# The weights of an instruction planner: ScalarE barred from the general PSUM banks after the first scores, and all work ordered anew

## What is computed

```
x = x + attn(layernorm(x))               # 16 heads, q and k made of 6 "line" coordinates, causal
x = x + xattn(layernorm(x), ctx, ctx)    # 16 heads of 16, 1601 context rows
x = x + ffn(layernorm(x))                # 16 experts, 64 rows each, chosen by a sinkhorn router

# attn:  q1,q2 = [x, x_prev] @ W1_q.T, W2_q.T;  k1,k2 = x @ W1_k.T, W2_k.T
#        q = lines(q1,q2); k = lines(k1,k2)   (6 products of pairs, normalised)
#        softmax(q . J k / sqrt(6), causal) @ (x Wv.T + bv), then @ Wo.T + bo
# xattn: softmax(q . k) @ v, then @ Wo.T + bo
```

## Time and profile before

| | |
|---|---|
| median of 3 executions | 1175.59 us (1175.5 to 1178.8) |
| the profiled execution | 1176.3 us, its span 1174.6 us |
| TensorE busy | 1102.7 us (94%) |
| VectorE busy | 854.1 us (73%) |
| ScalarE busy | 728.2 us (62%) |
| GpSimd busy | 153.5 us (13%) |
| mean granted TensorE clock | 0.979 of full speed |

### The profile page before, as it was taken

How to read it: one execution, slowest core, us unless ns; L and a number is a source line. 1 busy time by engine, 2 the same in 40 slices (tenths; PEclk the granted TensorE clock), 3 DMA queues, 4 the chain that set the end, 5 groups by cost and what they waited for, 6 DMA issues and landing times.

```text
span 1174.6 us, 30371 instructions
## 1 busy us (share of the span) xinstructions
PE 1102.7 (94%) x12600; PEld 522.4 (44%) x12600; DVE 854.1 (73%) x1998; ACT 728.2 (62%) x842; POOL 153.5 (13%) x260
## 2 busy tenths in 40 slices
PE   4898988999999999999999999999999999888997
PEld 2452432332332233554455455555654543466454
DVE  4986366588767788789788889788888891368631
ACT  0355756778777887677776887678875789310111
POOL 3134224112111111000001000010000000000522
PEclk9997998999999999999999999999999999999999
DMA  5112277502011000104231301111101000088696
GB/s 168 59 50 78 91 102 136 114 23 74 10 44 46 15 15 2 52 16 114 62 104 56 98 17 29 52 48 30 29 15 58 30 16 3 24 286 216 189 349 163
DMA packets 81561, 90.44 MB, mean 77 GB/s; under 512 B 18208, under 2 KB 73952, under 8 KB 81424
## 3 DMA queue, kind: packets, MB, share of 16 engines
q1 hardware_dynamic: 75264, 80.04, 24.5%
q10 hardware_dynamic: 4368, 6.29, 1.7%
q0 software_dynamic: 1792, 2.16, 1.0%
HBM read 73.42 MB, written 15.04 MB: 75 GB/s over the span
## 4 chain that ended last, share of the span: by engine, by line
PE 79%; DVE 13%; issue 3%; ACT 2%; DMA 2%; POOL 1%; SPq 0%; ACTq 0%; DVEq 0%
PE po L1778 24%; PE g L1886 16%; PE scores L1754 14%; PE scores L1758 6%; PE g L1871 3%; PE g L1977 2%; PE g L2001 2%; ACT probs L1194 2%; PE g L1861 2%; PE g L1821 1%; PE g L1865 1%; PE g L1806 1%; DMA xb<-x_d 1%; DVE mx L1465 1%; PE g L1831 1%
## 5 line engine op out<-in xcount | busy, mean ns | idle before, releaser
L1194 ACT ACTIVATE probs<-scores 128x1024 f32<-128x1024 f32 (+2 forms) x736 | 677.7, 968 | 226.1 <-PE scores L1754 132.6
L1465 DVE TENSOR_REDUCE mx<-g 128x1 f32<-128x400 f32 (+1 forms) x1024 | 526.1, 568 | 88.1 <-PE g L1886 79.3
L1886 PE MATMUL g<-cross_region,even_region 96*32 96x400 bf16 (+1 forms) x4096 | 305.7, 336 | 0.9 <-DVE mx L1465 0.4
L1754 PE MATMUL scores<-even_region,cross_region 99*32 99x512 bf16 (+1 forms) x3264 | 254.6, 379 | 3.0 <-ACT probs L1194 3.0
L1778 PE MATMUL po<-probs,cross_region 128*32 128x512 f32 (+1 forms) x1664 | 224.8, 594 | 0.8 <-ACT probs L1194 0.8
L1886 PEld LDWEIGHTS g<-cross_region,even_region 96*32 96x32 bf16 x4096 | 121.4, 95 | 172.8 <-DVE mx L1465 68.2
L1778 PE MATMUL po<-probs,self_region 128*32 128x512 f32 (+3 forms) x1280 | 153.4, 554 | 5.9 <-POOL probs L1055 5.0
L1754 PEld LDWEIGHTS scores<-even_region,cross_region 99*32 99x32 bf16 (+1 forms) x3264 | 100.1, 96 | 95.0 <-issue 41.7
L1758 PE MATMUL scores<-self_region 36*128 36x512 bf16 (+3 forms) x640 | 107.2, 360 | 7.2 <-ACT probs L1194 6.7
L1022 POOL TENSOR_TENSOR rstd<-mv,half 128x1 f32<-128x1 f32 x48 | 28.2, 592 | 549.2 <-DVE mv L1273 549.1
L1055 POOL TENSOR_SCALAR_AFFINE_SELECT probs<-probs 128x256 f32<-128x256 f32 x128 | 60.8, 482 | 237.7 <-ACT probs L1194 236.6
(11 more groups left out here) (288 smaller groups left out, 886.7 us busy)
## 6 DMA issues: line engine op xcount, KB each, us to landing
cross_region<-in_w SPq DMA_DIRECT2D x16, 1024.0 KB, 13.3
even_region<-xq_d SPq DMA_DIRECT2D x192, 64.0 KB, 2.3
self_region<-in_w ACTq DMA_DIRECT2D x6, 1024.0 KB, 7.0
self_region<-in_w SPq DMA_DIRECT2D x6, 1024.0 KB, 13.1
cross_region<-xk_d SPq DMA_DIRECT2D x24, 200.1 KB, 8.5
xb<-in_x SPq DMA_DIRECT2D x32, 128.0 KB, 2.8
xb<-x_d SPq DMA_DIRECT2D x32, 128.0 KB, 2.2
probs<-in_w SPq DMA_DIRECT2D x4, 1024.0 KB, 13.9
```

The source lines that it names most:

```text
L1194: act.activation(probs[0:rows, s % 4, :, off:], ps[s % 2][0:rows, :, off:], ACT.Exp, scale=LSCALE if QUADS[n][0] == "self" else 1.0).then_ ...
L1465: dve.reduce_max(mx[:, k % 2, b, h, c:c + 1], g[:, 0:n_keys], AX_X).then_inc(g_free, 1)
L1754: mm = pe.matmul(ps[s % 2][c:c + n_keys, a, :], k_cross[0:NS * DH + 3, h, i * P + c:i * P + c + n_keys], rhs, start=True, stop=True)
L1886: mm = pe.matmul(g[q:q + 32, 0:n_keys], q_max[k % 2][0:NS * DH, h, b * P + q:b * P + q + 32], k_cross[0:NS * DH, 4 * (k % 4) + h, start:st ...
```

## The change

Twelve numbers of `W` are new; nothing else differs. `act_late` goes from 0.3 to 50, and after the first score step VectorE empties every general bank. `hungry`, `act_near`, `max`, `max_end`, `lines`, `ctx`, `keys`, `weights`, `start`, `late` and `act_early` were chosen anew with it.

```diff
--- before.py
+++ after.py
@@ -69,10 +69,10 @@
 NS = len(Q_SLOTS)
 
 
-W = dict(hungry=0.714, fed=0.0083, act_near=0.2211, max=3.7538, max_ahead=0.0147, max_from=72.59, max_end=8.352,
-         prep=0.7203, x=0.2428, lines=0.6125, ctx=0.2601, keys=0.054, early_ctx=0.2835, early_lines=3.9514,
-         early_x=2.8, ones=0.4536, query=0.5762, weights=0.0015, start=1.7136, late=0.9073, act_late=0.3,
-         act_early=0.01)
+W = dict(hungry=0.2498, fed=0.0083, act_near=0.2255, max=0.4357, max_ahead=0.0147, max_from=72.59, max_end=10.0224,
+         prep=0.7203, x=0.2428, lines=0.1574, ctx=0.1821, keys=0.0688, early_ctx=0.2835, early_lines=3.9514,
+         early_x=2.8, ones=0.4536, query=0.5762, weights=0.0036, start=0.5141, late=1.0888, act_late=50,
+         act_early=0.0026)
 
 
 def build_plan():
```

## The result

| | before | after |
|---|---|---|
| median of 20 executions each | 1176.37 us (1172.9 to 1179.2) | 1172.22 us (1169.4 to 1175.2) |
| ratio, 95% interval | | 0.9967 [0.9958, 0.9976] |
| the profiled execution, its span | 1176.3, 1174.6 us | 1175.17, 1173.4 us |
| TensorE, VectorE, ScalarE busy | 1102.7, 854.1, 728.2 us | 1105.5, 860.9, 718.2 us |

The change makes the kernel 0.33% faster, some 4 us, with the bound of 0.3% inside the interval. The forecast was 1175, no change. The profiled execution of the changed kernel is the slowest of its twenty. So a second profile, of the same kernel run again, is read beside it; its span is 1168.9 us and its own time 1170.6. It errs the other way: it is the fastest of the eleven executions of its run, whose median is 1173.2.

The account below looks back on a forecast made before the run. TensorE was taken as the bound from 220.9 to 950 us, with idle time and lower clock to win or lose ahead of it. Terms +2.6 + 2.7 - 4.1 + 1.2 - 3.1 + 0.2 = -0.5 us gave 1175 us, range 1167 to 1183.

Parts of the forecast that it names:

- Ahead of the first scores: Up to the first scores: they come 2.7 us earlier, but some 5.2 us of TensorE work is left; net +2.6 us.
- Line blocks of tile 1: First scores to tile 1's line blocks: fewer filling steps leave TensorE idle 4.6 us in place of 1.9; +2.7 us.
- 86 to 160 us: `lines(2,0)` and `lines(2,1)` still slow the diagonal quads' masks, so the 3.5 us values wait stays; 0, ±3 us.
- 160 to 221 us: `lines(3,2)` ahead of the query cuts removes the 2.5 us line-block wait and 1.6 us of query-block waits; -4.1 us.
- rival 1: 160 to 220.9 us: all 8.5 us idle and the 5.1 us of lower clock go; 1166 us, chance 0.32.
- Quads 56 to 59: First `max` comes six quads late, so these quads, diagonal at the group's end, have no filling; +1.2 us.
- Changes of shape: 22 fewer changes of TensorE's tile shape: -3.1 us if TensorE is the bound at all, 0 if at none.
- The moved copies: Twelve steps' copies behind the first scores go from ScalarE to VectorE, neither on the path; 0, bounds -2 and +2 us.
- signs of being wrong: TensorE waits over 3 us for L1339, L1350 or L1432 (100-190 us), or pre-221 us lower clock over 8 us off 23.9.
- signs that it named for being right: Include a first L1854 wait of 3 us or more, the masks' wait still there, `max` starting within 3 us of 221.
- A: Theory of the experiments: the gain comes from where tile 3's steps now stand, around 160 to 220 us; ratio 0.997.
- C: Theory of the experiments: the gain comes from 22 fewer changes of TensorE's tile shape; ratio 0.997.

Follow-up runs that it names:

- b1: Kernel before with only `lines(3,2)` moved ahead of both query cuts on VectorE: ratio 0.9989 [0.9978, 1.0001] to before.
- a1: Changed kernel, order held, ScalarE again emptying the twelve listed `project`, `x_turn` and `ctx_v` banks: ratio 0.9991 [0.9975, 1.0006] to before.
- a3: Changed kernel, order held, only `project` 9 to 11 and two `x_turn` given back to ScalarE: ratio 0.9978 [0.9964, 0.9992] to before.
- e1: Changed kernel with, from quad 60, `max` steps between a self quad's two score steps put behind the second: ratio 0.9986 [0.9972, 1.0000] to before.
- d1: Planned with the weights of before until values step 36, the new weights from there: ratio 0.9979 [0.9961, 0.9998] to before.
- r0: Changed kernel run again unchanged, as the level for the others: 1173.19 against 1177.34 us, ratio 0.9970 [0.9960, 0.9981] to before.
- a2: Kernel before, order held, VectorE emptying the twelve listed `project`, `x_turn` and `ctx_v` banks: ratio 1.0104 [1.0085, 1.0123] to before.
- b2: Changed kernel with only `lines(3,2)` moved back behind both query cuts on VectorE: ratio 1.0005 [0.9992, 1.0019] to before.
- c1: Kernel before with only `act_late` raised from 0.3 to 50 and the order planned anew: ratio 1.0382 [1.0367, 1.0397] to before.
- d2: Planned with the new weights until values step 36, the weights of before from there: ratio 1.0108 [1.0092, 1.0124] to before.

## Where the prediction was right and wrong, step by step

The range of 1167 to 1183 held, and so did the forecast's own, 1171 to 1179. Its value, no change, did not: the sum said -0.5 us, the median moved by -4.2 and the second profile by -5.7. That it lies no further off is in part luck. At the last cross scores, up to which the sum counts, the second profile leads by 8.2 us, 7.7 more than the sum; behind them the scatter of the clock takes 2.5 us back, and most executions are slower than this one. By the prediction's own steps, with the table of lags:

- **Ahead of the first scores, +2.6: right.** Measured +3.0. The first scores stand at 65.3 us (64.7 forecast), the two waits are 5.2 and 4.2 us (5.3 and some 4).
- **Line blocks of tile 1, +2.7: the size held, the mechanism not.** The lag grows by 2.1 us up to quad 6, but not as a wait at L1854. `lines(1,2)` ends at 81.5 us as forecast, and TensorE comes there at the same moment. It had waited five times for exponentials and masks on the way, 2.6 us in all, and a clock of 0.89 between the scores of quads 0 and 6 in the second profile cost up to 1.8 us more; before, it was idle 2.2 us there at full clock. The sum had no term for that fall.
- **86 to 160 us, 0: the first step that failed.** "The 3.5 us wait of the values step stays where it is": it did not, and between quads 6 and 8 the lag shrinks by 4.8 us, of which 3.5 are this wait. `lines(2,0)` begins at 86.9 to 87.0 us on VectorE in all three profiles, while TensorE comes to quad 6 at 87.75 us before and at 81.5 after. So other masks fall beside it. Before, they are four in a row on GpSimd that take 6.0 us; in the second profile four later ones take 4.7, and in the first, one stands apart and three take 2.3. The wait of 2.0 us that is left in the second profile comes behind quad 8, where the lag grows again, by 3.1 us up to quad 24. The prediction went by the order of the steps and not by their times. Up to quad 44 the lag shrinks by 4.2 us in all, and TensorE is idle only 1.9 us less in this piece (8.5 against 10.4); the rest goes with the clock of 91.6 to 113.7 us, which b1 shows to scatter by 2.9 us.
- **160 to 221 us, -4.1: right in kind, much too small.** The waits for line parts and for blocks are gone but for 0.4 us. With them went the waits for exponentials, 2.5 us before and 0.4 in the second profile: 0.9 us of the 7.0 us idle remain. This is **the step that decided**. I kept the lower clock of the earlier trace rows in the sum and gave its end to rival 1, and it did end: over 192.6 to 220.9 us it is full in both profiles of after and in those of a1, a3 and e1, which share its order there. Between quads 44 and 60 after gains 6.5 us; without the step below it is 7.8, against the 2.5 us of the line parts and up to 5.1 us of clock that stood there. d1 parts the two: it keeps the wait, and the lower clock does not follow it but comes at 228 us; b1 loses the wait and keeps the lower clock. So, as far as one profile of each can tell, the clock is not tied to that wait.
- **Quads 56 to 59, +1.2: right.** The second profile shows three waits there, 0.24, 0.55 and 0.53 us, 1.3 in all. `max` begins at 224.9 us, 4 us behind the forecast's 221, since there are no steps to fill with until then.
- **Changes of shape, -3.1: near in size, the cause not shown.** The lag falls by 2.5 us between quads 60 and 137, where the new order has 15 changes fewer (2.1 us at the prediction's 0.14), and by 2.7 from quad 64 on, where it has 10 fewer (1.4 us); d1 gains 2.8 there with 11 fewer. So the price explains about half of it from quad 64 on. And e1 shows that it is no constant: 115 more changes saved gave nothing.
- **The moved copies, 0 (-2 to +2): too small.** In the new order it is worth 2.5 to 3.5 us (interval 1.6 to 5.2) that VectorE has them (a1 against r0); in the old order it costs 12 us (a2). The term counted the copies' time and had no clock in it: with the copies on ScalarE the new order runs at 0.81 behind the first scores (a1, a3) and not at 0.94.
- **What no term had:** 2.5 us are given back behind the last cross scores. Windows view from there to the end, before and then the second profile of after:

```profile
1008.10:1174.60 166.50, 141.17 (x814) 91.01 (x806) 88.27 (x263) 17.67 (x25) 31.82 (x39) 0.96 0.72 216
```

```profile
999.90:1168.90 169.00, 144.14 (x814) 93.03 (x806) 88.20 (x263) 17.69 (x25) 31.77 (x39) 0.94 0.70 213
```

The same 814 products take 3.0 us longer at a clock that is 0.02 lower (2 x 0.02 x 169 = 6.8 us more at the lower level, which cost at most 3.4). The first profile of after needs 168.9 us for this part too, but that of a1, with the order of after, only 165.6, and that of a2, with the order of before, 169.0. So it is scatter and no effect of the change.

Of its signs of being wrong, one came: behind the first scores and ahead of 221 us the lower clock takes 13.1 us in the first profile and 9.5 in the second instead of 23.9 (by the clocks of the windows above), over 8 us less. Three of the signs that it named for being right failed: the first L1854 has no wait, the masks' wait is not still there, and `max` starts 4 us behind 221 us. One copy of ScalarE (L1132) does come behind the first scores, at 67.5 us; it belongs to a product that stands ahead of them.

From 160 to 221 us the course was rival 1's in kind, "all of it goes, and with it the lower clock": of 8.5 us idle 1.8 remain, and the clock is full. In size it was not. Rival 1 gave 9.5 us more than the forecast, 1166 us in all, and the median came to 1172.2. The Trainium skill (TensorE: Matmul & The Clock Gate, What's actually happening) says that activity releases the full speed; the full clock over 192.6 to 220.9 us behind a stretch with 0.9 us idle agrees, and d1's full clock there behind 4.7 us idle, with 4.0 us idle in it, shows that this alone does not decide it.

**What stays open.** The place of `lines(3,2)` is needed for the gain (b2), and the new weights from quad 36 on keep two thirds of it (d1); so far A holds. But to hand the copies back in the new order takes most of the gain as well (a1). As each of the two takes nearly all of it, they do not add up as shares, and how they work together is not settled. C is argued from its size alone. Why b1 does not recover more is not settled either: in the old order the steps of tile 3 stand in the same stretch in which TensorE waits for exponentials, and no run moved those apart from `lines(3,2)`. That the masks' shorter wait came from its time alone was only argued from the traces.

## What to carry to other kernels

An assignment of copies to engines has no price of its own: to give the same twelve copies to VectorE costs 12 us in one order and gains some 3 in the other, so try such a change with the order replanned, and take it apart with the order held fixed. When a wait stands in front of a stretch with a low clock, give "the clock comes back" a term in the sum and not only a rival. And compare the lead at the same piece of work, corrected for the work not yet done: 9.1 us of apparent lead at quad 60 were 5.6. Then look for a second trace of the same order before a few us are given a cause: here two of them were 2.9 us apart by quad 24.

## What the runs showed of the hardware

- The granted clock scatters between executions of one kernel, and the time with it: the twenty of after go from 1169.4 us at 0.984 to 1175.2 us at 0.976. In the profiled one a fall to half speed stands in the stretch from 220.9 to 950 us, in which TensorE is busy 99% of the time. Windows of after, 400 to 434.3 us:

```profile
400.00:423.00 23.00, 21.51 (x262) 6.91 (x260) 19.03 (x43) 18.44 (x22) 3.26 (x8) 1.00 0.01 2
423.00:434.30 11.30, 11.30 (x84) 2.77 (x84) 5.90 (x12) 5.11 (x6) 0.00 (x0) 0.55 0.14 37
```

  The second profile has 140 products and a clock of 1.00 over the same 11.3 us, behind the same 1.5 us idle. One such fall costs some 5 us, more than the whole effect of the change. A single profile is therefore no measure of a 0.3% change.
- A stretch in which TensorE counts as busy nearly all the time can be at the lower clock: 0.61 in c1 (busy 47.6 of 52 us) and 0.63 in d2 (26.7 of 28 us), both while it runs at VectorE's pace on short products.
- Two chips differ by more than the change: before takes 1177 us on two of them and 1186 on a third, so each kernel is compared with before on the same chip. The part behind the last cross scores takes 177 to 181 us on the third in three profiles, and 166 to 169 in the ten others.
